# A graph-attention layer on one core: one penalty row a chunk for both segment scans, columns transposed from a broadcast source, and a fourth message tile on VectorE

## What is computed

```python
deg = maximum(segment_sum(ones(E), dst, N), 1.0)
h = maximum(_layernorm(x), 0.0)
q = (h @ Wq + bq).reshape(N, DH, NH)
k = (h @ Wk + bk).reshape(N, DH, NH)          # v = k
scores = einsum('edh,edh->eh', q[src], k[dst])
m = segment_max(scores, src)                   # over all edges of a source node
ex = exp(scores - m[src])
attn = ex / segment_sum(ex, src)[src]
msgs = attn[:, None, :] * k[dst]
x = x + segment_sum(msgs, src).reshape(N, 512) @ Wo + bo
h = maximum(_layernorm(x), 0.0)
agg = segment_sum(h[src], dst)
x = x + h @ W1.T + b1 + (agg / deg[:, None]) @ W2.T + b2
```

## Time and profile before

| | |
|---|---|
| median of 3 runs | 2015.37 us (2011.95 to 2026.04) |
| profiled execution | 2021.78 us |
| its span, first to last instruction | 2020.0 us |
| mean granted clock of TensorE | 0.942 |
| busy of the span | PE 81%, DVE 71%, POOL 57%, ACT 47% |

### The profile page before, as it was taken

How to read it: one execution, slowest core, us unless ns; L and a number is a source line. 1 busy time by engine, 2 the same in 40 slices (tenths; PEclk the granted TensorE clock), 3 DMA queues, 4 the chain that set the end, 5 groups by cost and what they waited for, 6 DMA issues and landing times.

```text
span 2020.0 us, 23951 instructions
## 1 busy us (share of the span) xinstructions
PE 1640.1 (81%) x5635; PEld 952.9 (47%) x5635; DVE 1426.0 (71%) x2720; ACT 949.0 (47%) x3673; POOL 1144.9 (57%) x1322
## 2 busy tenths in 40 slices
PE   0378884058888989888988888795999999999998
PEld 0133332036666666666666666442444444444443
DVE  9899997888888889898989887267344434444441
ACT  6111110148999999999999999242000000000000
POOL 2000000077878887887878783012777777777772
PEclk9989987579999999999999999898999999999999
DMA  3212221266565656565565652854777777777673
GB/s 122 65 57 71 69 63 50 73 185 171 147 187 157 191 159 190 163 181 166 173 174 164 187 159 74 195 152 121 211 213 219 212 223 213 217 214 213 201 208 94
DMA packets 129584, 318.42 MB, mean 158 GB/s; under 512 B 38108, under 2 KB 38358, under 8 KB 129428
## 3 DMA queue, kind: packets, MB, share of 16 engines
q0 software_dynamic: 70240, 229.93, 39.6%
q1 hardware_dynamic: 59188, 86.80, 14.6%
HBM read 280.81 MB, written 35.86 MB: 157 GB/s over the span
## 4 chain that ended last, share of the span: by engine, by line
PE 38%; DVE 30%; issue 14%; DMA 13%; SPq 2%; DVEq 1%; POOL 1%; ACT 1%; another core or an unknown queue 0%; POOLq 0%; ACTq 0%
PE sums L728 11%; PE wide L684 10%; PE wide L756 8%; PE sums L825 7%; DMA node<-h2tab 6%; DMA out<-node 5%; DVE arena L964 4%; DVE arena L963 4%; DVE nodes L1252 2%; DMA h2tab<-node 2%; DVE nodes L1198 1%; DVE nodes L1243 1%; DVE node L1141 1%; DVE q_win L1059 1%; DVE q_win L1057 1%
## 5 line engine op out<-in xcount | busy, mean ns | idle before, releaser
L553 ACT ACTIVATE nodes<-arena,nodes 128x64 f32<-128x64 f32 x2840 | 682.7, 332 | 0.0
L468 POOL DMA_INDIRECT arena<-ktab,idx x425 | 425.8, 1002 | 182.0 <-issue 114.2
L468 POOL DMA_INDIRECT arena<-h2tab,idx x425 | 445.4, 1048 | 140.5 <-issue 133.8
L684 PE MATMUL wide<-w_sb,node 128*125 128x512 f32 x1000 | 473.1, 622 | 51.3 <-DVEq L1075 36.6
L728 PE MATMUL sums<-nodes,oh 128*125 128x260 f32 x1768 | 463.6, 405 | 42.9 <-DVE nodes L1198 42.9
L728 PEld LDWEIGHTS sums<-nodes,oh 128*125 128x125 f32 x1768 | 339.8, 197 | 118.5 <-DVE nodes L1198 54.3
L825 PE MATMUL sums<-arena,oh 128*125 128x512 f32 x850 | 374.5, 598 | 7.4 <-DMA arena<-h2tab,idx 7.4
L684 PEld LDWEIGHTS wide<-w_sb,node 128*125 128x125 f32 x1000 | 190.6, 197 | 280.7 <-issue 252.7
L756 PE MATMUL wide<-q_win,node 125*128 125x512 bf16 x1275 | 311.5, 382 | 6.0 <-issue 6.0
L633 ACT ACTIVATE node<-wide 128x500 f32<-128x500 f32 x51 | 28.9, 586 | 584.1 <-PE wide L811 584.1
L1243 DVE TENSOR_TENSOR nodes<-wide,arena 128x1024 f32<-128x1024 f32 (+1 forms) x225 | 258.6, 1158 | 12.9 <-PE wide L756 12.2
(11 more groups left out here) (187 smaller groups left out, 1161.5 us busy)
## 6 DMA issues: line engine op xcount, KB each, us to landing
node<-node_tab SPq DMA_DIRECT2D x27, 531.2 KB
q_win<-qtab SPq DMA_DIRECT2D x26, 375.0 KB
qtab<-q_win SPq DMA_DIRECT2D x25, 375.0 KB
arena<-ktab,idx POOLq DMA_INDIRECT x425, 5.5
arena<-h2tab,idx POOLq DMA_INDIRECT x425, 4.7
node<-h2tab SPq DMA_DIRECT2D x26, 250.0 KB
nodes<-x SPq DMA_DIRECT2D x1, 6250.0 KB
ktab<-node SPq DMA_DIRECT2D x25, 250.0 KB
```

Of the source, the lines that this page charges most:

```text
L468: gp.indirect_dma_start(rows[:, b, t, :], None, tab, bass.IndirectOffsetOnAxis(ap=idx[:, b, t:t + 1], axis=0)).then_inc(s["rows_in"][b][PA ...
L553: last = act.activation(msgs[:, t, h // HH, h % HH * DH:(h % HH + 1) * DH], rows[:, 1 - b, t, h * DH:(h + 1) * DH], ACT.Copy, scale=den_in ...
L684: last = pe.matmul(out, ncol[:, b, c, :], w_sb[:, w, c, :], start=start and c == 0, stop=stop and c == KC - 1)
```

## The change

The two penalty rows of a chunk become one: `links[:, b]` holds 8 x 17 + 1 numbers, and entry s is the penalty between positions s-1 and s. The forward scan reads entries 0 to 135 and the backward scan entries 1 to 136. The entries at the heads' borders stay at the -1e30 that they are filled with once. `whole` goes: TensorE transposes from the value in `sides_pen`, read eight times by a stride of zero. `flags` is left with 7 instructions instead of 10. VectorE forms the messages of four tiles instead of three and ScalarE those of 13 instead of 14, and the first two parts of the row buffer become four and three tiles.

```diff
-        pen = scratch[:, 0:4 * SEGS].rearrange("p (b k h t) -> p b k h t", b=2, k=2, h=H)
+        links = scratch[:, 0:2 * (SEGS + 1)].rearrange("p (b s) -> p b s", b=2)
...
-        whole = scratch[:, AT + 7 * CT + 1:AT + 7 * CT + 1 + 4 * H].rearrange("p (b k h) -> p b k h", b=2, k=2)
-        ROWS_AT = AT + 7 * CT + 1 + 4 * H
+        ROWS_AT = AT + 7 * CT + 1
...
-        PARTS = [(0, 3), (3, 4), (7, 5), (12, CT - 12)]
+        PARTS = [(0, 4), (4, 3), (7, 5), (12, CT - 12)]
...
-        MT = 3
+        MT = 4
+        WHOLE = (CT - 1, 0)
...
-                    last = pe.transpose(whole_turn[:, k, :], whole[:, b, k, :], ident[:, :])
+                    last = pe.transpose(whole_turn[:, k, :], sides_pen[:, b, k, WHOLE[k]:WHOLE[k] + 1].to_broadcast([128, H]), ident[:, :])
...
-                st = Steps(flag_step, g, 10)
+                st = Steps(flag_step, g, 7)
...
-                st.mark(dve.tensor_copy(pen[:, b, 0, :, 1:CT], inside))
-                st.mark(dve.tensor_copy(pen[:, b, 1, :, 0:CT - 1], inside))
-                st.seen(6)
-                st.mark(dve.tensor_copy(whole[:, b, 0, :], sides_pen[:, b, 0, CT - 1:CT].to_broadcast([128, H])))
-                st.then(dve.tensor_copy(whole[:, b, 1, :], sides_pen[:, b, 1, 0:1].to_broadcast([128, H])))
+                st.mark(dve.tensor_copy(links[:, b, 0:SEGS].rearrange("p (h t) -> p h t", h=H)[:, :, 1:CT], inside))
+                st.seen(7)
                 st.end()
...
-                      (scratch[:, 0:4 * SEGS], -BIG), (from_left[:, :, :], -BIG), (from_right, -BIG)]
+                      (links[:, :, :], -BIG), (from_left[:, :, :], -BIG), (from_right, -BIG)]
...
-                st.then(dve.tensor_tensor_scan(line(seg_max), line(pen[:, b, 0, :, :]), line(sc), -BIG, ALU.add, ALU.max))
-                st.then(dve.tensor_tensor_scan(line(over)[:, ::-1], line(pen[:, b, 1, :, :])[:, ::-1], line(seg_max)[:, ::-1], -BIG, ALU.add, ALU.max))
+                st.then(dve.tensor_tensor_scan(line(seg_max), links[:, b, 0:SEGS], line(sc), -BIG, ALU.add, ALU.max))
+                st.then(dve.tensor_tensor_scan(line(over)[:, ::-1], links[:, b, 1:SEGS + 1][:, ::-1], line(seg_max)[:, ::-1], -BIG, ALU.add, ALU.max))
```

## The result

The changed kernel takes 2047.4 us in the median of 6 runs (2043.7 to 2053.0), the kernel before 2018.3 (2012.0 to 2026.0). The ratio is 1.0144 with an interval of 1.0116 to 1.0172: 29 us slower, where 8 were forecast. The profiled execution has a span of 2051.1 us; before it was 2020.0.

What follows compares the result with a forecast made beforehand. VectorE's queue was taken to bound the attention stage. The fourth tile's +13.4 us and the flags' -5.2 us sum to +8.2 us on the 2015.4 us median: 2024 us, 0.4% slower, range 2012 to 2042.

Steps and rivals of the forecast that it cites:

- VectorE's queue sets the chunk time: Attention stage: VectorE's own instructions, run end to end, set the 32.8 us chunk; ScalarE, GpSimd and TensorE wait for it.
- The rival that ScalarE was the bound: Attention stage: ScalarE's queue paces everything, so 1.93 us less work a chunk makes it faster, 1975 us; chance 0.06.
- The fourth tile costs 0.54 us a chunk with no cover: VectorE's two message instructions (L1198) grow from 957 to 1225 ns each; 25 chunks x 0.54 = 13.4 us slower.
- The flags save 0.43 us, in about half of the chunks: Three fewer VectorE copies between scans and carry; counts in the 12 chunks where TensorE waits at L773, 5.2 us gained.
- The 0.26 us estimated from the Trainium skill's page: Alternative price of the three removed copies in flags: 12 x 0.26 = 3.1 us gained, the whole 2 us slower.
- The rest costs nothing: Broadcast load of the L745 transposes, offset reverse scan, smaller fill and aggregation's first gather part: nothing, at most 1.3 us once.
- The pause before the messages grows to 1.75 us and the clock stays up: TensorE's wait before the first messages grows from 1.2 to about 1.75 us on average, with no second clock fall.
- 1.75 is nearer to 1.7 than to 2.2: Argument against a clock fall at the messages: a 1.7 us pause brought none, L768's 2.2 us did about every second time.
- The prediction's own signs of this rival: For TensorE's clock falling at the messages: granted clock 0.50 after the message wait, or L1240 wait well over 0.4 us a chunk.
- The price, 2.7 us a chunk that falls: Cost of a TensorE clock fall at the messages, from VectorE's 2.70 us wait for scores in the stage's first chunk.
- Falls in five chunks or more, 0.14, 2051 with ten: TensorE's clock falls a second time, at the messages: over 1% slower from 5 chunks, 2051 us with ten; chance 0.14.

Runs made afterwards that it cites:

- flags-only run: Kernel before with only the new single penalty row and 7 instructions in flags, three message tiles kept on VectorE: 2014.8 us, ratio 0.9971.

## Why the prediction was wrong, point by point

- *VectorE's queue sets the chunk time.* Right. ScalarE lost 1.9 us of work a chunk and only its wait grew, from 1.2 to (114.3 - 14.0) / 24 = 4.2 us; nobody gained by it. The rival that ScalarE was the bound is out.
- *The fourth tile costs 0.54 us a chunk with no cover.* Right: 2 x 263 ns, and turns without a fall agree.
- *The flags save 0.43 us, in about half of the chunks.* Right in size (L1163 to L1261 is 0.45 us in the chunk shown, against 0.89) and in place, as the flags-only run shows. The 0.26 us estimated from the Trainium skill's page (VectorE: DVE Perf Modes) was too small. In the rows the starts of the three removed copies lie 0.14, 0.13 and 0.08 us behind the starts before them, and the last one took 0.29 us where L1163, now the last, takes 0.22; the 0.24 us of waiting behind the last copy stay. The trace was the better guide.
- *The rest costs nothing.* Right. The load from the broadcast source takes 87 ns in the median, the same as the load of eight real columns before.
- *The pause before the messages grows to 1.75 us and the clock stays up.* The first half is right, 1.8 on average; the second is the step that failed, "1.75 is nearer to 1.7 than to 2.2". It set the average of the new pauses beside the longest of the old ones. The old average of 1.2 us held short pauses, in turns with a fall behind the scans, and usual ones of 1.35; the usual ones went to 1.84 and more, in 19 of 24 turns, and 15 of these were followed by a fall. That a pause of 1.7 us brings none was read rightly: no pause under 1.8 us did in any undisturbed trace. The rows compared should have been the usual ones: from 1.35 to 1.84. The prediction's own signs of this rival are there, too: a clock of 0.50 right behind the message wait, and a wait at L1240 of 34.9 / 25 = 1.4 us a chunk.
- *The price, 2.7 us a chunk that falls.* Too high: 1.71 measured. The row that it came from was the stage's first chunk, where the clock was low before the messages too.
- *Falls in five chunks or more, 0.14, 2051 with ten.* This rival happened, with 15 falls: 2015.4 + 15 x 1.71 + 8.2 would give 2049, and 2047 was measured; its own price of 2.7 would have given 2064, so that its 2051 for ten falls came close is luck, too few falls at too high a price. The mechanism, its place and its sign were there; the chance was not. The passage of the Trainium skill named beside it (TensorE: Matmul & The Clock Gate, "HAM oscillation") speaks of a clock that falls again in each turn of a loop. The trace agrees in kind: the fall came back in 15 of 24 turns. But the waits of the page's example are 3 to 5 us long, and here 1.84 us was enough.

## What to carry to other kernels

Where an engine in line with the bound gets longer, look at what its partner does meanwhile: half a microsecond more of waiting cost TensorE its clock in 15 turns, and each of those turns lost 1.71 us to it, three times the 0.53 us of the work. Before counting a pause as harmless, look at the pauses one by one and not at their average: the short ones pulled the average under what most turns would have. And signal in smaller steps: releasing the same four tiles two by two took back nearly all of the loss for 0.14 us of instructions.

## What the runs showed of the hardware that was not expected

- TensorE's clock fell from 2.4 to 1.2 GHz behind pauses of 1.84 us and more before the messages: 58 of 78 pauses from 1.81 us on had a fall behind them, and none of 138 up to 1.76 us. In a kernel with a mean pause of 1.8 us that made 13 to 15 of 24 turns, at 1.5 three, at 1.3 or less none.
- The falls come in rows. Before, those behind the scans came in 14 of 24 turns, never in more than two that follow each other; in the changed kernel those behind the messages come in up to three that do (turns 1 to 3, 13 to 15, 17 to 19 and 21 to 23, counted from 0). What sets this is not shown.
- Idle work can pay: 250 matmuls whose result nobody reads (25 chunks, 10 each) made the changed kernel 17 us faster.
